# Causal attention in a transformer block: the order of the key tiles, and on diagonal steps both scores and the mask first

## The chip, the cores and the metric

One core of one Trainium2 chip. The metric is the device time of one launch in microseconds (us), lower is better. The core's engines run their own instruction streams and meet at semaphores: TensorE (PE, with its weight loads shown apart as PEld), VectorE (DVE), ScalarE (ACT), GpSimd (POOL) and SyncE (SP), which issues most of the DMAs.

## The reference, cut to what matters

Two batches of 2048 rows of 512 numbers pass a pre-norm block: attention with 16 heads of width 32 over a latent of 128, then a mixture of experts. Only the attention core is touched:

```python
scores = jnp.einsum('bhqd,bhkd->bhqk', q, k) / jnp.sqrt(jnp.float32(DH))
causal = jnp.tril(jnp.ones((s, s), dtype=bool))
scores = jnp.where(causal[None, None], scores, -jnp.inf)
attn = jax.nn.softmax(scores, axis=-1)
out = jnp.einsum('bhqk,bhkd->bhqd', attn, v)
```

## The kernel before, in words

Six phases follow each other: projections, attention, output projection with the shared expert, routing, experts, and combination. `phase_attention` is the one that changes.

**Units and steps.** Eight iterations (two batches, four groups of four heads) each have four units, one for each query chunk q = 0 to 3 of 512 queries. A unit goes through its key tiles kt of 128 keys: tiles below 4q are full, tiles 4q to 4q+3 lie on the diagonal, where tile number d = kt - 4q concerns only the queries from 128d on (512, 384, 256 and 128 columns). Each tile takes two steps, p = 0 and p = 1, for two head pairs. So there are 640 steps, 256 of them diagonal.

**A step on PE.** A step n computes two scores (keys x queries, one for each head of the pair, `score(n, 0)` and `score(n, 1)`) into a ring of three PSUM banks: score number i waits for the exponential of number i-3. On full tiles both exponentials wait only for their score. On diagonal tiles VectorE first adds a triangle to 128 columns of both scores (`mask(n)`), and both exponentials wait for that mask. In odd steps PE also multiplies the exponentials of an earlier tile with the values (`values`, four matmuls side by side, one and a half steps behind); in even steps, for some tiles, it adds up the exponentials with a matrix of ones (`count_ones`, two tiles behind). For the other tiles (`POOL_TILES`) GpSimd adds them up instead, and `finish` brings its sum into PSUM two or four steps into the next unit.

**The maxima.** The softmax subtracts a maximum of each row, which has to be known before the unit's first score. So for coming units PE computes scores the other way round, one *item* (a matmul into one of three other PSUM banks), VectorE takes its maximum, and when a unit's maxima are all there PE transposes them ("turn"), ScalarE copies the rows and SP's DMA puts them beside the queries. 1280 such items are laid over the steps by `attention_plan`: each step gets "room" for the PE work that the planner counts in it, and items are handed out in proportion. A step's items fall into three parts (`item_shares`). The order within a step before the change:

| engine | order in step n |
|---|---|
| PE | score(n,0), first third of the items, ones or values, second third, score(n,1), last third, finish |
| DVE | maxima of the first two thirds, mask(n), maxima of the last third |
| ACT | turn rows if any, exp(n,0), exp(n,1), output and sums of the unit before |

Each engine takes its stream strictly in this written order; PE therefore stands still where the next matmul in its stream has to wait.

Of the kernel before, what the change touches and what calls it, by code (L numbers as in the profile page):

```python
# [21 lines left out]
TPC = CH // P  # L22
# [337 lines left out]
NG = BATCH * GPB  # L360
HG = 4
PAIRS = 2
NQ = SEQ // CH
SCALE = 1.0 / DH ** 0.5


POOL_TILES = ((), (0, 1, 2, 4, 5), (0, 1, 2, 4, 5, 7, 8), (0, 1, 2, 4, 5, 7, 8, 10, 11, 12))
FINISH = (2, 4, 4, 2)
KRING = 6


def attention_steps():

    units = [(it, q) for it in range(NG) for q in range(NQ)]
    steps, first_step = [], []
    for u, (it, q) in enumerate(units):
        first_step.append(len(steps))
        steps += [(u, q, kt, p) for kt in range(TPC * (q + 1)) for p in range(PAIRS)]
    first_step.append(len(steps))
    return units, steps, first_step  # L380


def key_chunk_before(it, j):
# [5 lines left out]
def attention_plan(units, steps, first_step):  # L389

    stream, pending, turn_at = [], None, {}
    for u, (it, q) in enumerate(units):
        items = [("max", u, t, h, c) for t in range(TPC) for h in range(HG) for c in range(q + 1)]
        lag = 4
        stream += items[:lag]
        if pending is not None:
            turn_at[pending] = len(stream)
            stream.append(("turn", pending))
        stream += items[lag:]
        pending = u  # L400
    turn_at[pending] = len(stream)
    stream.append(("turn", pending))

    def cost(item):
        if item[0] == "turn":
            return 500
        _, u, t, h, c = item
        return 150 + min(CH, (TPC * units[u][1] + t + 1) * P - c * CH)

    def room(n):  # L410
        u, q, kt, p = steps[n]
        width = CH - max(kt - TPC * q, 0) * P
        work = 2 * max(width, 2 * P) + 100 * (kt >= TPC * q)
        if p:
            work += 4 * width
        elif kt not in POOL_TILES[q]:
            work += 4 * width
        return work

    costs = [cost(i) for i in stream]  # L420
    total = [0]
    for x in costs:
        total.append(total[-1] + x)
    rooms = [0]
    for n in range(len(steps)):
        rooms.append(rooms[-1] + room(n))

    released = []
    for u, (it, q) in enumerate(units):
        at = 0  # L430
        if it:
            at = first_step[u - NQ + 1] + 5
            kb = key_chunk_before(it, q)
            if kb is not None:
                at = max(at, first_step[NQ * kb[0] + NQ - 1] + 2 * TPC * (kb[1] + 1) + 5)
        released.append(at)
    due = [max(first_step[u] - 6, 0) for u in range(len(units))]
    start = turn_at[0] + 1
    upto, pos = [], start
    for n in range(len(steps)):  # L440
        slope = 0.0
        for u in range(len(units)):
            if turn_at[u] >= pos:
                slope = max(slope, (total[turn_at[u] + 1] - total[pos]) / max(rooms[due[u]] - rooms[n], 1400))
        upto_cost = slope * (rooms[n + 1] - rooms[n]) + (total[pos] if n == 0 else carry)
        while pos < len(stream) and total[pos] + costs[pos] / 2 < upto_cost:
            if stream[pos][0] == "max" and released[stream[pos][1]] > n:
                upto_cost = total[pos]
                break
            pos += 1  # L450
        carry = upto_cost
        upto.append(pos)
    turn_step = {}
    for n in range(len(steps)):
        for i in range(upto[n - 1] if n else start, upto[n]):
            if stream[i][0] == "turn":
                turn_step[stream[i][1]] = n
    for u in range(1, len(units)):
        assert turn_step[u] < first_step[u], (u, turn_step[u], first_step[u])
    return stream, start, upto, turn_at, turn_step  # L460
# [38 lines left out]
def phase_attention(nc, x, w, scratch, ahead):  # L499
# [37 lines left out]
    def pool_count(n):  # L537

        u, q, kt, p = steps[n]
        if kt == POOL_TILES[q][0]:  # L540
            n += PAIRS * (POOL_TILES[q][1] - POOL_TILES[q][0])
        return pool_ops.index(n) + 1

    def pool_total(u):
# [22 lines left out]
    with ExitStack() as ctx:  # L567
# [52 lines left out]
        with nc.Block() as block:  # L620
            @block.gpsimd
            def _(g):
# [11 lines left out]
                for i, n in enumerate(pool_ops):  # L634
                    u, q, kt, p = steps[n]
                    f = summed.index(u)
                    out = acc[f % 2][:, 2 * p:2 * p + 2]
                    lo = max(kt - TPC * q, 0) * P
                    so_far = out
                    if kt == POOL_TILES[q][1]:  # L640
                        so_far = pt[(n - PAIRS * (kt - POOL_TILES[q][0])) % NPB][:]
                        if f >= 2:
                            g.wait_ge(s_fin, f - 1)
                    else:
                        g.wait_ge(s_add, i - 1)
                    g.wait_ge(s_exp, 2 * n + 2)
                    if kt == POOL_TILES[q][1]:
                        assert lo == 0
                    g.tensor_tensor(out[:, :, lo:], so_far[:, :, lo:], pt[n % NPB][:, :, lo:], ALU.add).then_inc(s_add, 1)  # L649

            @block.sync
            def _(sp):
# [55 lines left out]
                for n in range(NS):  # L708
                    u, q, kt, p = steps[n]
                    it = units[u][0]  # L710
                    if n and kt == 0 and p == 0:
                        jt, j = units[u - 1]
                        if jt + 1 < NG:
                            sp.wait_ge(s_st, 2 * n)
                            load_q(jt + 1, j)
                        later = NQ * jt + j + KRING
                        if j == NQ - 1 and later < NG * NQ:
                            load_k(*divmod(later, NQ))
                    if q == NQ - 1 and kt % TPC == 0 and p == 0 and kt:
                        later = NQ * it + kt // TPC - 1 + KRING  # L720
                        if later < NG * NQ:
                            sp.wait_ge(s_st, 2 * n)
                            load_k(*divmod(later, NQ))
                    for s in range(NU):
                        if turn_step.get(s) == n:
                            turn_rows(s)
                    at = n - 4
                    if at >= 0:
                        vu, vq, vkt, vp = steps[at]
                        if vq == NQ - 1 and vkt % TPC == TPC - 1 and vp and units[vu][0] + 1 < NG:  # L730
                            sp.wait_ge(s_pv, (at + 1) // 2)
                            load_v(units[vu][0] + 1, vkt // TPC)
                    done = unit_ending(n, 3)
                    if done is not None:
                        store_out(done)
# [26 lines left out]
            def _(v):  # L762
# [36 lines left out]
                        ins.then_inc(s_msk, 1)  # L799

                for n in range(NS):
                    here, _, some, there = item_shares(n)
                    for i in range(here, some):
                        if stream[i][0] == "max":
                            partial_max(i)
                    if steps[n][2] >= TPC * steps[n][1]:
                        mask(n)
                    for i in range(some, there):
                        if stream[i][0] == "max":
                            partial_max(i)  # L810
                    if n == first_step[NQ * NG - 2]:
# [59 lines left out]
            def _(pe):  # L871
# [27 lines left out]
                def score(n, j):  # L899
# [3 lines left out]
                    lo = min(max(d, 0) * P, 2 * P)  # L903
                    if 2 * n + j >= NST:
                        pe.wait_ge(s_exp, 2 * n + j - NST + 1)
                    if kt == 0 and p == 0 and j == 0:
                        pe.wait_ge(s_row[q], 16 * (it + 1))
                    at = key_slot(it, kt // TPC) * CH + kt % TPC * P
                    h = 2 * p + j
# [3 lines left out]
                def values(m):  # L913
# [1 line left out]
                    it = units[u][0]  # L915
                    lo = max(kt - TPC * q, 0) * P
                    pe.wait_ge(s_exp, 4 * m + 4)
                    if kt == 0 and u:
                        pe.wait_ge(s_oev, u)
                    if q == kt // TPC and kt % TPC == 0:  # L920
                        pe.wait_ge(s_v[q], 16 * (it + 1))
                    for h in range(HG):
                        ins = pe.matmul(ob[h * DH:(h + 1) * DH, lo:], vbuf[:, kt, h * DH:(h + 1) * DH],  # L923
                                        pt[(2 * m + h // 2) % NPB][:, h % 2, lo:],
                                        start=(kt == 0), stop=(kt == TPC * q + TPC - 1))
                    ins.then_inc(s_pv, 1)

                def count_ones(m):
# [1 line left out]
                    if kt in POOL_TILES[q]:  # L930
                        return
                    lo = max(kt - TPC * q, 0) * P
                    begin = min(k for k in range(TPC * (q + 1)) if k not in POOL_TILES[q])
                    if kt == begin and u:
                        pe.wait_ge(s_sev, u)
                    for h in range(HG):
                        ins = pe.matmul(sb[h * DH:(h + 1) * DH, lo:], ones[:],  # L937
                                        pt[(2 * m + h // 2) % NPB][:, h % 2, lo:],
                                        start=(kt == begin), stop=(kt == TPC * q + TPC - 1 and not POOL_TILES[q]))
                    ins.then_inc(s_one, 1)  # L940

                def finish(u):
# [10 lines left out]

                for n in range(NS):
                    here, *some = item_shares(n)
                    score(n, 0)
                    for i in range(here, some[0]):
                        item(i)
                    if n % 2 == 0 and n >= 4:
# [2 lines left out]
                        values((n - 3) // 2)  # L962
                    for i in range(some[0], some[1]):
                        item(i)
                    score(n, 1)
                    for i in range(some[1], some[2]):
                        item(i)
                    done = unit_ending(n, FINISH)
# [942 lines left out]
```

## Time and profile before

| | |
|---|---|
| time, median of 3 runs | 2658.76 us (2655.09 to 2663.19) |
| the profiled execution | 2654.73 us, its span 2652.8 us |
| attention steps, first score to last exponential | 296 to 1486 us of the span |
| PE, weight loads, DVE, ACT, POOL busy over the span | 2338.7, 1478.8, 1560.3, 1053.6, 999.8 us |
| mean granted TensorE clock | 0.935 of full speed |

Busy time of an engine is the union of its instructions. The end of a matmul is modelled, so the PE is called busy for a while after it could take the next. "PEclk" in a row is the granted share of full clock in that stretch.

### The profile page before, as it was taken

The page shows a single profiled execution, that of the slowest core. Times are in us where ns is not written, and L with a number is a line of the kernel's source. Part 1 is how long each engine was busy: PE and PEld are TensorE (multiplying, and loading weights), DVE is VectorE, ACT ScalarE, POOL GpSimd, SP SyncE. Part 2 cuts the span into 40 slices and gives each one's busy share as a digit, 9 for nine tenths or more (in the row PEclk, how much of TensorE's full clock was granted, in tenths as well). Part 3 has the DMA queues.
Part 4 walks back from the last instruction along what each step waited for, and adds up shares of the span by engine and source line. Part 5 has one row for each costly group of instructions (what it writes and reads, how often), then busy time and mean ns, then how long its engine had stood idle before and what let it go on. Part 6 is the DMA issues. An engine that isn't in the chain of part 4 may idle for free. (4 is left out here: it accounts for less than half of the span.)

```text
span 2652.8 us, 34530 instructions
## 1 busy us (share of the span) xinstructions
PE 2338.7 (88%) x12088; PEld 1478.8 (56%) x12088; DVE 1560.3 (59%) x3220; ACT 1053.6 (40%) x1928; POOL 999.8 (38%) x592
## 2 busy tenths in 40 slices
PE   5997699999999999999999699999489999999950
PEld 5775344444444444444443377776467777777740
DVE  3664787667676777766674444443645555555535
ACT  2332155565555555555656422221033333333310
POOL 0000067474656566573746633130221111112036
PEclk8998599899999999998999899999589999999975
DMA  3766512213131313322110234341245454545349
GB/s 100 279 234 231 124 28 65 65 49 74 39 81 33 82 31 80 102 65 65 49 47 27 63 105 143 111 143 48 69 151 178 139 171 146 167 154 160 113 157 381
DMA packets 178740, 301.72 MB, mean 114 GB/s; under 512 B 23616, under 2 KB 65728, under 8 KB 178624
## 3 DMA queue, kind: packets, MB, share of 16 engines
q1 hardware_dynamic: 159360, 242.54, 30.1%
q0 software_dynamic: 14656, 49.29, 5.9%
q10 hardware_dynamic: 4608, 8.39, 0.8%
q8 instruction: 66, 1.08, 0.2%
q14 instruction: 50, 0.41, 0.1%
HBM read 199.65 MB, written 100.27 MB: 113 GB/s over the span
## 5 line engine op out<-in xcount | busy, mean ns | idle before, releaser
L832 ACT ACTIVATE b_pt<-b_st 128x512 f32<-128x512 f32 (+3 forms) x1280 | 620.8, 533 | 489.3 <-PE b_st L910 208.3
L773 DVE TENSOR_REDUCE b_mpart<-b_mx 128x1 f32<-128x512 f32 x768 | 510.2, 685 | 209.2 <-PE b_mx L889 207.4
L649 POOL TENSOR_TENSOR b_acc<-b_acc,b_pt 128x1024 f32<-128x1024 f32 (+1 forms) x256 | 593.4, 2344 | 73.3 <-ACT b_pt L832 73.0
L910 PE MATMUL b_st<-b_q,b_k 97*128 97x512 f32 (+2 forms) x1280 | 497.9, 405 | 71.9 <-ACT b_pt L832 57.9
L889 PE MATMUL b_mx<-b_k,b_q 96*128 96x512 f32 (+2 forms) x1280 | 514.5, 418 | 30.7 <-DVE b_mt L781 25.9
L889 PEld LDWEIGHTS b_mx<-b_k,b_q 96*128 96x128 f32 x1280 | 250.4, 197 | 306.7 <-DVE b_mpart L773 138.6
L910 PEld LDWEIGHTS b_st<-b_q,b_k 97*128 97x128 f32 x1280 | 244.2, 193 | 262.9 <-ACT b_pt L832 228.7
L923 PE MATMUL b_ob<-b_pt,b_v 128*32 128x512 f32 (+3 forms) x2560 | 305.7, 550 | 1.1 <-ACT b_pt L832 1.1
L770 DVE CUSTOM_DVE_ANT_0 b_unread<-b_mx,b_later 128x384 bf16<-128x384 f32 (+3 forms) x512 | 244.6, 483 | 77.9 <-PE b_mx L889 77.4
L649 POOL TENSOR_TENSOR b_acc<-b_pt 128x1024 f32<-128x1024 f32 x48 | 113.4, 2378 | 443.8 <-ACT b_pt L832 443.7
L61 PE MATMUL e_fb<-e_xh,e_w_guh 128*128 128x512 f32 (+1 forms) x552 | 219.6, 398 | 1.5 <-DVE e_xl L1730 1.5
L63 PE MATMUL e_fb<-e_xl,e_w_guh 128*128 128x512 f32 (+1 forms) x552 | 217.5, 394 | 0.0
L62 PE MATMUL e_fb<-e_xh,e_w_gul 128*128 128x512 f32 (+1 forms) x552 | 217.3, 394 | 0.0
L1702 ACT ACTIVATE e_sg<-e_fb 128x512 f32<-128x512 f32 (+1 forms) x69 | 41.1, 596 | 341.2 <-PE e_fb L63 341.2
L1674 POOL COPY e_idx<-token 128x4 uint32 (+1 forms) x23 | 4.2, 184 | 410.9 <-PE e_tb L1764 410.9
L1735 DVE TENSOR_TENSOR e_hf<-e_sg,e_fb 128x512 f32<-128x512 f32 (+1 forms) x69 | 47.3, 686 | 189.1 <-ACT e_sg L1702 189.1
L794 DVE TENSOR_TENSOR b_st<-b_st,b_sooner 128x256 f32<-128x256 f32 x170 | 72.9, 429 | 80.8 <-PE b_st L910 79.3
L937 PE MATMUL b_sb<-b_pt,b_ones 128*32 128x512 f32 (+3 forms) x1152 | 117.2, 481 | 0.0
L63 PEld LDWEIGHTS e_fb<-e_xl,e_w_guh 128*128 128x128 f32 (+1 forms) x552 | 98.8, 179 | 29.5
L61 PEld LDWEIGHTS e_fb<-e_xh,e_w_guh 128*128 128x128 f32 (+1 forms) x552 | 98.9, 179 | 29.2 <-issue 1.8
L1677 POOL DMA_INDIRECT e_xg<-scr_xn,e_idx x92 | 100.1, 1088 | 39.8 <-issue 21.0
L62 PEld LDWEIGHTS e_fb<-e_xh,e_w_gul 128*128 128x128 f32 (+1 forms) x552 | 98.8, 179 | 27.8
(224 smaller groups left out, 3524.2 us busy)
## 6 DMA issues: line engine op xcount, KB each, us to landing
scr_y<-e_y SPq DMA_DIRECT2D x23, 1024.0 KB, 5.0
b_q<-scr_qh SPq DMA_DIRECT2D x64, 256.0 KB, 4.4
b_k<-scr_kh SPq DMA_DIRECT2D x64, 256.0 KB, 4.0
e_gu<-in_L_ffn_w_gate_dram SPq DMA_DIRECT2D x23, 704.0 KB, 6.4
e_gu<-in_L_ffn_w_up_dram SPq DMA_DIRECT2D x23, 704.0 KB, 7.7
e_d<-in_L_ffn_w_down_dram SPq DMA_DIRECT2D x23, 512.0 KB, 7.7
a_xin<-in_L_attn_x_dram POOLq DMA_DIRECT2D x8, 1024.0 KB, 5.9
scr_qh<-a_qh SPq DMA_DIRECT2D x8, 1024.0 KB, 4.6
```

Source lines behind the costliest of these rows:

```text
L61: nc.tensor.matmul(out, wh, xh, start=first, stop=False)
L62: nc.tensor.matmul(out, wl, xh, start=False, stop=False)
L63: return nc.tensor.matmul(out, wh, xl, start=False, stop=last)
L649: g.tensor_tensor(out[:, :, lo:], so_far[:, :, lo:], pt[n % NPB][:, :, lo:], ALU.add).then_inc(s_add, 1)
L770: v.tensor_tensor_reduce(unread[i % NMX][:, 0:w], mxb[i % NMX][:, 0:w], later[:, CH - w:], 1.0, -3e38, ALU.add, ALU.max, part).then_inc(s_ ...
L773: v.tensor_reduce(part, mxb[i % NMX][:, 0:w], AX.X, ALU.max).then_inc(s_red, 1)
L832: act.activation(pt[n % NPB][:, j, lo:], stb[:, (2 * n + j) % NST, lo:], ACT.Exp, scale=SCALE).then_inc(s_exp, 1)
L889: ins = pe.matmul(bank[:, 0:max(w, 2 * P)], qb[0:KR, h, q * CH + t * P:q * CH + (t + 1) * P], kb[0:KR, h, at:at + max(w, 2 * P)], start=Tr ...
L910: pe.matmul(stb[:, (2 * n + j) % NST, lo:], kb[:, h, at:at + P], qb[:, h, q * CH + lo:(q + 1) * CH], start=True, stop=True).then_inc(s_st, 1)
L923: ins = pe.matmul(ob[h * DH:(h + 1) * DH, lo:], vbuf[:, kt, h * DH:(h + 1) * DH], pt[(2 * m + h // 2) % NPB][:, h % 2, lo:], start=(kt == ...
L937: ins = pe.matmul(sb[h * DH:(h + 1) * DH, lo:], ones[:], pt[(2 * m + h // 2) % NPB][:, h % 2, lo:], start=(kt == begin), stop=(kt == TPC * ...
L1677: g.indirect_dma_start(out=xg[n][:, t, :], in_=scratch["xn"], out_offset=None, in_offset=bass.IndirectOffsetOnAxis(ap=idx[n][:, t:t + 1], ...
```

## The change: what it does

1. The diagonal tiles no longer stand at the end of a unit but are put between full ones, by a written list `ORDER`. Everything that asked for the first or last tile, or for the distance of two tiles, now asks for the place in that list. The tiles whose sums PE makes are listed in `ONES_TILES`; GpSimd still adds the same number of tiles in each unit, with the same widths.
2. SP's loads into the key and value buffers of a chunk are issued when the last tile of that chunk has been used in the new order (`steps_to_leave`: after steps 10, 20, 30 and 32 of a unit with q = 3, instead of 8, 16, 24 and 32).
3. On diagonal steps PE issues score(n,1) directly behind score(n,0), ahead of the items and of ones or values.
4. VectorE applies mask(n) ahead of all maxima of step n.

```diff
-POOL_TILES = ((), (0, 1, 2, 4, 5), (0, 1, 2, 4, 5, 7, 8), (0, 1, 2, 4, 5, 7, 8, 10, 11, 12))
+ORDER = ((0, 1, 2, 3), (0, 1, 4, 2, 5, 3, 6, 7), (0, 1, 2, 8, 3, 4, 9, 5, 6, 10, 7, 11),
+         (0, 1, 2, 12, 3, 4, 5, 13, 6, 7, 8, 14, 9, 10, 11, 15))
+ONES_TILES = ((0, 1, 2, 3), (2, 6, 7), (2, 9, 6, 10, 11), (2, 4, 13, 8, 14, 15))
+POOL_TILES = tuple(tuple(kt for kt in ORDER[q] if kt not in ONES_TILES[q]) for q in range(NQ))
...
-        steps += [(u, q, kt, p) for kt in range(TPC * (q + 1)) for p in range(PAIRS)]
+        steps += [(u, q, kt, p) for kt in ORDER[q] for p in range(PAIRS)]
...
+def steps_to_leave(j):
+    return PAIRS * (1 + max(ORDER[NQ - 1].index(kt) for kt in range(TPC * j, TPC * (j + 1))))
...
                 for n in range(NS):
-                    here, _, some, there = item_shares(n)
-                    for i in range(here, some):
-                        if stream[i][0] == "max":
-                            partial_max(i)
+                    here, _, _, there = item_shares(n)
                     if steps[n][2] >= TPC * steps[n][1]:
                         mask(n)
-                    for i in range(some, there):
+                    for i in range(here, there):
                         if stream[i][0] == "max":
                             partial_max(i)
...
                     here, *some = item_shares(n)
+                    diag = steps[n][2] >= TPC * steps[n][1]
                     score(n, 0)
+                    if diag:
+                        score(n, 1)
                     for i in range(here, some[0]):
                         item(i)
...
-                    score(n, 1)
+                    if not diag:
+                        score(n, 1)
```

## Rows read from the trace of the kernel before

**Rows 1.** Every engine, in the attention steps (lengths and busy us, count; clock; DMA)

```profile
296.00:1486.00 1190.00, 1123.01 (x6548) 517.47 (x6552) 811.88 (x2128) 663.32 (x1373) 705.84 (x304) 0.97 0.22 55
```

**Rows 2.** Iteration 4: q = 0, then full and diagonal stretch of q = 1, 2, 3

```profile
core 0: us, PE busy (x) PEld busy (x) DVE busy (x) ACT busy (x) POOL busy (x), PEclk, DMA share, GB/s
911.09:926.59 15.50, 14.75 (x104) 6.30 (x103) 11.82 (x31) 7.10 (x18) 0.00 (x0) 1.00 0.58 137
926.59:940.79 14.20, 13.62 (x86) 6.78 (x86) 9.12 (x23) 9.82 (x20) 7.31 (x4) 1.00 0.29 75
940.79:954.05 13.26, 11.43 (x71) 5.31 (x70) 10.56 (x26) 6.27 (x15) 10.42 (x5) 1.00 0.01 1
954.05:982.29 28.24, 28.24 (x162) 12.57 (x161) 19.45 (x42) 18.59 (x35) 19.93 (x9) 1.00 0.15 38
982.29:997.37 15.08, 13.30 (x86) 6.46 (x85) 10.69 (x42) 6.76 (x16) 8.35 (x4) 1.00 0.01 2
997.37:1041.61 44.24, 44.24 (x255) 20.41 (x255) 29.41 (x82) 28.40 (x53) 33.34 (x15) 1.00 0.29 73
1041.61:1055.60 13.99, 11.53 (x72) 5.43 (x70) 11.15 (x29) 6.27 (x15) 8.94 (x4) 1.00 0.34 76
```

**Rows 3.** The same columns: full stretch of q = 2 in iterations 1, 2 and 6

```profile
510.65:544.38 33.73, 33.73 (x162) 15.39 (x162) 20.32 (x43) 18.91 (x35) 19.93 (x9) 0.81 0.13 33
659.25:691.92 32.67, 32.67 (x163) 14.86 (x162) 20.31 (x42) 18.63 (x35) 19.92 (x9) 0.84 0.13 33
1242.49:1275.34 32.85, 32.85 (x163) 14.99 (x163) 20.23 (x42) 18.63 (x35) 19.92 (x9) 0.83 0.13 33
```

**Rows 4.** Waits in the attention steps (us in total, times, longest)

```profile
ACT b_pt L832 <- DVE b_st L794: 178.4, 153, 18.9
...
PE b_st L910 <- ACT b_pt L832: 57.9, 90, 1.3
```

**Rows 5.** Groups by shape (count | busy us, mean ns | idle before)

```profile
L773 DVE TENSOR_REDUCE b_mpart<-b_mx 128x1 f32<-128x512 f32 x768 | 510.2, 685 | 209.2 <-PE b_mx L889 207.4
L832 ACT ACTIVATE b_pt<-b_st 128x512 f32<-128x512 f32 x896 | 497.0, 599 | 300.3 <-PE b_st L910 208.3 <-DVE b_st L794 59.2 <-DVE b_st L798 23.6
...
L832 ACT ACTIVATE b_pt<-b_st 128x128 f32<-128x128 f32 x128 | 28.6, 275 | 56.7 <-DVE b_st L794 35.2 <-DVE b_st L798 20.1 <-PE b_sb L937 1.4
```

**Rows 6.** Timeline, iterations 2 and 3: narrow diagonal steps (start, length, instruction, idle before)

```profile
761.94 0.28 PE L910 MATMUL b_st<-b_q,b_k 97*128 97x256 f32 x1
...
762.75 0.42 DVE L794 TENSOR_TENSOR b_st<-b_st,b_sooner 128x256 f32<-128x256 f32 x1
...
763.72 0.39 PE L910 MATMUL b_st<-b_q,b_k 97*128 97x256 f32 x1 [0.42 <-ACT b_pt L832]
...
764.15 0.50 DVE L798 TENSOR_TENSOR b_st<-b_st,b_sooner 128x128 f32<-128x128 f32 x2 [0.51 <-PE b_st L910]
...
764.76 0.45 ACT L832 ACTIVATE b_pt<-b_st 128x128 f32<-128x128 f32 x2 [0.82 <-DVE b_st L798]
...
765.09 0.39 PE L910 MATMUL b_st<-b_q,b_k 97*128 97x256 f32 x1
...
765.86 0.64 PE L937 MATMUL b_sb<-b_pt,b_ones 128*32 128x256 f32 x8
...
766.43 0.19 PEld L889 LDWEIGHTS b_mx<-b_k,b_q 96*128 96x128 f32 x1 [0.41 <-issue]
```

**Rows 7.** Timeline, iteration 3: tile 12 and the start of tile 13

```profile
896.20 0.63 PE L910 MATMUL b_st<-b_q,b_k 97*128 97x512 f32 x2
...
896.99 0.43 DVE L794 TENSOR_TENSOR b_st<-b_st,b_sooner 128x256 f32<-128x256 f32 x1
...
897.59 1.06 PE L923 MATMUL b_ob<-b_pt,b_v 128*32 128x512 f32 x8
898.58 0.19 PEld L889 LDWEIGHTS b_mx<-b_k,b_q 96*128 96x128 f32 x1 [0.84 <-DVE b_mpart L773]
...
900.61 0.44 PE L910 MATMUL b_st<-b_q,b_k 97*128 97x384 f32 x1 [0.78 <-ACT b_pt L832]
```

More of the change, by code:

```diff
@@ L434, in attention_plan @@
             if kb is not None:
-                at = max(at, first_step[NQ * kb[0] + NQ - 1] + 2 * TPC * (kb[1] + 1) + 5)
+                at = max(at, first_step[NQ * kb[0] + NQ - 1] + steps_to_leave(kb[1]) + 5)
         released.append(at)
@@ L540, in pool_count @@
         if kt == POOL_TILES[q][0]:
-            n += PAIRS * (POOL_TILES[q][1] - POOL_TILES[q][0])
+            n += PAIRS * (ORDER[q].index(POOL_TILES[q][1]) - ORDER[q].index(POOL_TILES[q][0]))
         return pool_ops.index(n) + 1
@@ L640, in _ @@
                     if kt == POOL_TILES[q][1]:
-                        so_far = pt[(n - PAIRS * (kt - POOL_TILES[q][0])) % NPB][:]
+                        so_far = pt[(n - PAIRS * (ORDER[q].index(kt) - ORDER[q].index(POOL_TILES[q][0]))) % NPB][:]
                         if f >= 2:
@@ L710, in _ @@
                     it = units[u][0]
-                    if n and kt == 0 and p == 0:
+                    if n and n == first_step[u]:
                         jt, j = units[u - 1]
@@ L718, in _ @@
                             load_k(*divmod(later, NQ))
-                    if q == NQ - 1 and kt % TPC == 0 and p == 0 and kt:
-                        later = NQ * it + kt // TPC - 1 + KRING
-                        if later < NG * NQ:
+                    for j in range(NQ - 1):
+                        if q == NQ - 1 and n == first_step[u] + steps_to_leave(j) and NQ * it + j + KRING < NG * NQ:
                             sp.wait_ge(s_st, 2 * n)
-                            load_k(*divmod(later, NQ))
+                            load_k(*divmod(NQ * it + j + KRING, NQ))
                     for s in range(NU):
@@ L729, in _ @@
                         vu, vq, vkt, vp = steps[at]
-                        if vq == NQ - 1 and vkt % TPC == TPC - 1 and vp and units[vu][0] + 1 < NG:
-                            sp.wait_ge(s_pv, (at + 1) // 2)
-                            load_v(units[vu][0] + 1, vkt // TPC)
+                        for j in range(NQ):
+                            if vq == NQ - 1 and at + 1 == first_step[vu] + steps_to_leave(j) and units[vu][0] + 1 < NG:
+                                sp.wait_ge(s_pv, (at + 1) // 2)
+                                load_v(units[vu][0] + 1, j)
                     done = unit_ending(n, 3)
@@ L905, in score @@
                         pe.wait_ge(s_exp, 2 * n + j - NST + 1)
-                    if kt == 0 and p == 0 and j == 0:
+                    if n == first_step[u] and j == 0:
                         pe.wait_ge(s_row[q], 16 * (it + 1))
@@ L917, in values @@
                     pe.wait_ge(s_exp, 4 * m + 4)
-                    if kt == 0 and u:
+                    if kt == ORDER[q][0] and u:
                         pe.wait_ge(s_oev, u)
@@ L924, in values @@
                                         pt[(2 * m + h // 2) % NPB][:, h % 2, lo:],
-                                        start=(kt == 0), stop=(kt == TPC * q + TPC - 1))
+                                        start=(kt == ORDER[q][0]), stop=(kt == ORDER[q][-1]))
                     ins.then_inc(s_pv, 1)
@@ L932, in count_ones @@
                     lo = max(kt - TPC * q, 0) * P
-                    begin = min(k for k in range(TPC * (q + 1)) if k not in POOL_TILES[q])
+                    begin = ONES_TILES[q][0]
                     if kt == begin and u:
@@ L938, in count_ones @@
                                         pt[(2 * m + h // 2) % NPB][:, h % 2, lo:],
-                                        start=(kt == begin), stop=(kt == TPC * q + TPC - 1 and not POOL_TILES[q]))
+                                        start=(kt == begin), stop=(kt == ORDER[q][-1] and not POOL_TILES[q]))
                     ins.then_inc(s_one, 1)
```

## The prediction

> **What bounds the kernel now.** I read the busy shares of the attention steps first, then stretches of one iteration, then the waits, then the timeline inside single steps. Only the attention steps are touched: 1190 of the 2652.8 us of span [rows 1]. There PE is busy 1123 us, VectorE 812, GpSimd 706, ScalarE 663 [rows 1]: PE sets the pace, and its 67 us without work are the plain stock that a better order could give back. Iteration 4, undisturbed, shows where they lie [rows 2]: nothing in the full stretches of q = 2 and 3, 0.58 us in that of q = 1, 0.75 in q = 0, and 1.83, 1.78 and 2.46 us in the diagonal stretches. Diagonal tiles cost 3.3 to 3.8 us each there, full ones 3.5 to 3.7, though the diagonal ones are narrower. The waits say why: ScalarE waits 178 us for the mask on two score banks, and PE waits 57.9 us, in 90 places, for an exponential before a score [rows 4]. The rest of PE's idle time is mostly the 12 us before the first row of maxima arrives, and the change doesn't touch that.
>
> The Trainium skill (Trainium Kernel Development and Optimization, "Reading a trace") calls the busy time of matmuls a bad measure and that of weight loads a good one. By it the stock is larger than 67 us, since weight loads are busy 517 of 1190 us; no row says how much larger, and the sum below does not use it.
>
> **The chain behind one wait.** In a run of narrow diagonal steps it is seen bare [rows 6]: a second score starts at 763.72, the mask at 764.15, the exponential at 764.76, and the score that reuses the bank at 765.09. That is 1.37 us with an exponential of 0.28 us (128 columns), so 1.09 us plus the exponential. From 0.28 to 0.60 us for 128 and 512 columns [rows 5], in even steps, the chain is 1.37, 1.47, 1.58 and 1.69 us for d = 3, 2, 1, 0. It gets longer if VectorE is still at maxima (0.69 us each [rows 5]) when the scores come: score to mask is 0.43 us bare, 0.81 us in the pair 761.94 and 762.75 [rows 6], and 0.56 us for tile 12 (its second score 0.23 us behind 896.20) [rows 7]. I take 0.35 us on top wherever a full tile with three items stands ahead; bounds are 0 and one maximum, 0.69.
>
> **Where the wait stands, before and after.** Between score(n,1) and score(n+1,1) PE has work that covers the chain. Before, from p = 0 to p = 1 that work holds the values, 1.0 us (897.59 to 898.58 [rows 7]), and the chain is hidden; from p = 1 to the next tile's p = 0 it holds only the next score and one or two items at 0.25 us, and PE stands (0.78 us at 900.61 [rows 7]), except where ones fall into that step. After, both scores stand at the head. From p = 1 onward the values follow them, and a full tile comes next: hidden. But from p = 0 to p = 1 there remain only the items of p = 0 and the next score. So the wait isn't removed, it changes places: one per diagonal tile.
>
> **The sum for a diagonal tile after**: own score issue (0.23, 0.18, 0.12, 0.12 us by width; 0.23 us apart in [rows 7], narrower ones in proportion) twice, the chain, the items of p = 1 at 0.25, and the values at 1.0, since a full tile's values now fall there. The planner's own costs and rooms, gone through by hand for the new order, give p = 1 of the diagonal tiles 3, 2, 1, 1 items for q = 1 and 3 and 2, 2, 3, 1 for q = 2.
> - q = 3: 0.23 + 2.04 + 0.23 + 0.75 + 1.0 = 4.25 for d = 0; 3.79, 3.31 and 3.21 for d = 1, 2, 3: 14.6 us, against 13.99.
> - q = 2: 4.0 + 3.79 + 3.81 + 3.21 = 14.8, against 15.08.
> - q = 1: 4.25 + 3.79 + 3.31 + 2.43 = 13.8, against 13.26 (tile 7 follows tile 6, so its chain is bare and its values take 0.57 us, as the 256 columns of 765.86 to 766.43 [rows 6]).
> Together 43.2 against 42.3 us [rows 2]: +0.8 us an iteration.
>
> What moves to the full stretches: values of diagonal tiles, narrower by 0.65 us (q = 2, 3) and 0.2 us (q = 1), -1.5; ones, +0.35, +1.8 and +1.0, since tile 2 and most ones of diagonal tiles now run there, less 1.15 that leaves the first steps of the next unit; some three items from the diagonal stretch of q = 2, +0.85. That is +1.3 us. With the diagonal part +2.1 us an iteration, +17 us over eight. The last unit has no items, so neither backlog nor cover; I leave it as the others.
>
> **q = 0** keeps its order, all steps diagonal; only parts 3 and 4 act. 15.5 us with VectorE 11.8 busy [rows 2]. Tiles 0 and 1 stay near VectorE's work and `finish`, tiles 2 and 3 go down to the chain: 0.8 us a unit, seven units, -6 us. The first unit's burst of items is VectorE's either way.
>
> **The clock.** Three full stretches of q = 2 take 33.7, 32.7 and 32.9 us at a granted clock of 0.81 to 0.84, against 28.24 at 1.00 in iteration 4 [rows 2, 3]. Parts of them ran at 1.2 instead of 2.4 GHz; that costs 14.5 us in all, and each follows q = 1's diagonal stretch, where PE has idled. After, q = 1's tiles 6 and 7 still stand together with two waits of about 1 us. I count -4; bounds are -15 (no dip left) and +23 (a dip in all eight). By the Trainium skill (TensorE: Matmul & The Clock Gate, "The HAM clock gate") idleness drops the clock to half and sustained work brings it back; the trace agrees as to the order of events.
>
> **What costs nothing.** GpSimd adds as many tiles, equally wide. In q = 3 its last run of three (9, 10, 11) starts some 17 us before `finish` (four tiles of 3.6 us, then a tile of the next unit) and takes six additions of 2.4 us (33.34 us in 15 records of the full stretch [rows 2]), 14.3 us: hidden by some 3 us; uncovered it would cost up to 3 us in each iteration. SP's chunk loads start 2 to 6 steps later, 4 to 11 us, are used in the next iteration, and nothing urgent is queued behind them: the row DMA of step 17 lies between those of steps 10 and 20. The two row turns that move one step later (q = 1 and 3) still precede their unit by more than 10 us. The masks number the same; behind a waiting mask on VectorE stand that step's maxima, behind those PE's items three banks on. VectorE, at 11.15 of 13.99 us [rows 2], has room.
>
> **Sum**: 2654.7 (profiled) + 17 - 6 - 4 = 2661.7. The median of the runs is 4.0 us above the profiled execution, so about **2666 us**.
>
> **Rivals.**
> - *The masks get in at once.* The 0.35 us goes for some 80 tiles (-28), and with spread waits the dips go too (-11): 2627. For: VectorE takes no maximum ahead of the mask any more, and only 0.13 us of delay shows at tile 12 [rows 7]. Against: the previous p = 1 step issues its last item just ahead of the diagonal scores.
> - *VectorE becomes late*, the other mechanism that ends slower. Waiting in line for two scores at every mask, it loses about 0.45 us a step of p = 0 and 1 (192 steps outside q = 0), while two or three items wait behind. It decides once VectorE's 11.15 us plus eight such waits, 3.6, exceed the stretch's 14.6: just there. If half of it reaches PE, +43: 2709.
> - *More clock dips.* One wait per tile in q = 1 after the rows' turn leaves PE idle in a third of the tiles; dips in all units would give 2666 + 27 = 2693. Against: full stretches between waits have no idle time at all.
>
> **How the numbers follow.** Likeliest, 0.48: the waits change places, 2645 to 2685. Masks at once, 0.27: 2605 to 2645. VectorE late, 0.15: 2685 to 2730. Clock, 0.10: 2675 to 2700. No change means within 0.3%, 2650.8 to 2666.7. The likeliest case splits into 0.09 faster, 0.25 same, 0.14 slower. So faster 0.36, same 0.25, slower 0.39. For 8 in 10: 2618 to 2702.
>
> **What would show it.** The wait of PE's scores for exponentials: about 88 times, longest at d = 0 (about 1.2 us), all in front of p = 1's second score, none in full tiles. Diagonal tiles of q = 3 at 4.2, 3.8, 3.3 and 3.2 us. If the score-to-mask time is 0.43 in p = 0, the first rival holds; if PE's items wait for maxima in diagonal tiles, the second. The prediction is wrong if the diagonal tiles of an iteration lose over 3 us together: then the cover I counted from the values and ones is larger than it is, or the backlog of maxima smaller.

## The result and the profile after

The changed kernel takes 2709.65 us (median of 4 runs, 2701.75 to 2711.5) against 2660.98 us for the kernel before: a ratio of 1.0175, 95% interval 1.0146 to 1.0205. It is slower by 48.7 us. The forecast was 2666 us, with 2618 to 2702 as its range.

The attention steps after the change, the row that answers to [rows 1]:

```profile
296.00:1526.00 1230.00, 1140.59 (x6542) 523.40 (x6540) 816.38 (x2127) 671.29 (x1372) 700.63 (x302) 0.96 0.21 53
```

Both rows start at 296 us, but the first score stands at 294.53 us here and at 296.51 us before. From there to the last exponential the steps take 1231.8 us instead of 1189.1: 43 us more. PE idles 89 us in the row instead of 67. Every engine executes as many instructions as before, but PE is also busy 18 us longer with them. The granted clock (0.96 for 0.97) goes with that; by the clock records of the two traces PE ran at the lower of its two levels, 1.2 instead of 2.4 GHz, for 91 us of the attention steps, and for 70 before.

By iteration, from first score to first score (the last one to the last exponential), with the granted clock of that stretch (the third kernel is the first of the experiments):

| iteration | 0 | 1 | 2 | 3 | 4 | 5 | 6 | 7 |
|---|---|---|---|---|---|---|---|---|
| before, us | 170.0 | 149.4 | 149.3 | 145.8 | 144.5 | 143.1 | 149.8 | 137.0 |
| its clock | 0.92 | 0.95 | 0.97 | 0.99 | 1.00 | 1.00 | 0.95 | 0.99 |
| changed, us | 183.8 | 151.1 | 148.5 | 150.0 | 155.5 | 148.9 | 151.9 | 141.9 |
| its clock | 0.88 | 0.98 | 1.00 | 0.99 | 0.95 | 1.00 | 0.98 | 0.95 |
| tile order alone, us | 174.2 | 143.7 | 143.6 | 143.7 | 143.7 | 145.1 | 144.3 | 138.9 |
| its clock | 0.90 | 1.00 | 1.00 | 1.00 | 1.00 | 0.99 | 1.00 | 0.95 |

So an iteration at full clock loses 4.0 to 5.8 us, and iteration 0 alone, with its long stretch at the lower clock, loses 14.

The span grew by 47.3 us, from 2652.8 to 2700.1. The attention starts 2 us earlier and lasts 42.7 us longer, so 6.6 us lie behind it, where no line was changed. 4.2 of them are a wait that the tile order makes. The last unit has no unit behind it, so its `finish` runs straight after the last tile, and GpSimd now adds tile 11 just ahead of tile 15. PE waits for that sum; in the changed kernel and then before:

```profile
1531.79 1.94 PE L950 MATMUL b_sb<-b_acc,b_ones 128*32 128x512 f32 x8 [4.81 <-POOL b_acc L657]
```

```profile
1486.92 1.95 PE L945 MATMUL b_sb<-b_acc,b_ones 128*32 128x512 f32 x8
```

From the last exponential to this matmul it is 5.5 us instead of 1.35. The inner order alone, whose tile order is the old one, has 0.95 us there, and the tile order alone has 4.64. What makes the other 2.4 us stays open; behind this matmul the profiled executions of the kernels here differ by up to 6 us among themselves.

Where PE waits, as in [rows 4], to the end of the attention steps; the third row is PE waiting for a maximum:

```profile
ACT b_pt L837 <- DVE b_st L802: 152.9, 163, 12.0
...
PE b_st L915 <- ACT b_pt L837: 83.0, 123, 1.8
...
PE b_mx L894 <- DVE b_mpart L781: 3.4, 8, 1.9
```

PE's scores wait 83 us for exponentials, 123 times, against 57.9 us and 90 times [rows 4]. Sorted by place, 65 us of it in 86 places stand in front of the second score of p = 1 in diagonal tiles of q = 1 to 3, 8 us in 8 places in front of p = 0's there, 7.5 us in 22 places in q = 0, and 2 us in other places. PE hardly ever waits for a maximum.

Iteration 5 after the change, undisturbed at full clock, in the columns of [rows 2]: q = 0, 1, 2, 3.

```profile
1083.57:1099.13 15.56, 14.47 (x96) 6.30 (x97) 12.38 (x31) 6.79 (x17) 3.35 (x2) 1.00 0.94 205
1099.13:1128.34 29.21, 25.73 (x154) 12.06 (x154) 19.44 (x48) 16.71 (x36) 17.70 (x8) 1.00 0.47 138
1128.34:1174.43 46.09, 42.25 (x255) 19.67 (x255) 31.43 (x85) 25.99 (x53) 27.70 (x12) 1.00 0.09 25
1174.43:1232.50 58.07, 55.59 (x323) 26.09 (x324) 39.61 (x107) 34.73 (x69) 39.64 (x18) 1.00 0.26 64
```

Against [rows 2] (15.50; 14.20 + 13.26 = 27.46; 43.32; 58.23) q = 0 and q = 3 are unchanged; q = 1 loses 1.75 us and q = 2 loses 2.8. Against the same iteration of the kernel before, also at full clock (15.57, 27.41, 42.83, 57.32 us), they lose 0, 1.8, 3.3 and 0.75 us. The diagonal tiles themselves, in the order 4, 5, 6, 7, then 8, 9, 10, 11, then 12, 13, 14, 15, with their sum:

```profile
1106.03:1110.51 4.48, 3.62 (x18) 1.43 (x17) 2.93 (x8) 3.11 (x7) 4.48 (x3) 1.00 1.12 296
1114.39:1118.22 3.83, 3.00 (x17) 1.39 (x16) 2.32 (x6) 2.16 (x5) 2.05 (x2) 1.00 0.00 0
1122.14:1125.44 3.30, 2.73 (x17) 1.21 (x15) 2.93 (x8) 1.51 (x4) 3.30 (x2) 1.00 0.00 0
1125.44:1128.34 2.90, 1.86 (x15) 1.07 (x15) 1.79 (x5) 0.86 (x5) 0.18 (x1) 1.00 0.00 0
1139.80:1143.99 4.19, 3.11 (x17) 1.40 (x15) 2.56 (x7) 2.37 (x5) 1.19 (x1) 1.00 0.00 0
1151.27:1155.30 4.03, 3.10 (x18) 1.52 (x17) 3.23 (x8) 2.16 (x5) 4.03 (x3) 1.00 0.00 0
1162.90:1167.48 4.58, 2.93 (x20) 1.48 (x18) 1.95 (x11) 2.89 (x7) 0.00 (x0) 1.00 0.01 2
1171.09:1174.43 3.34, 3.16 (x24) 1.28 (x22) 2.60 (x8) 1.49 (x5) 3.34 (x2) 1.00 0.02 7
1185.39:1189.80 4.41, 3.46 (x19) 1.62 (x18) 2.88 (x10) 2.73 (x5) 1.55 (x1) 1.00 0.00 0
1200.25:1204.22 3.97, 3.97 (x24) 1.48 (x23) 2.89 (x9) 1.79 (x4) 3.61 (x2) 1.00 0.02 4
1215.22:1218.65 3.43, 2.65 (x17) 1.25 (x15) 2.79 (x8) 1.70 (x5) 0.53 (x1) 1.00 0.51 130
1229.10:1232.50 3.40, 2.65 (x16) 1.14 (x15) 2.56 (x7) 1.49 (x5) 3.40 (x2) 1.00 0.61 148
sum 45.86, PE 36.25 PEld 16.27 DVE 31.43 ACT 24.25 POOL 27.67; mean PE 3.02 PEld 1.36 DVE 2.62 ACT 2.02 POOL 2.31
```

The reader sees PE idle 0.6 to 1.65 us in ten of the twelve diagonal tiles. In tile 13, in whose p = 0 step 1.0 us of ones (those of tile 4) falls, PE never idles, and in tile 11, which has the narrower ones of tile 10 there, only 0.2 us. The worst is tile 10. Its timeline:

```profile
1162.50 0.68 PE L901 MATMUL b_mx<-b_ident,b_mt 128*97 128x128 f32 x4
...
1163.21 0.60 ACT L843 ACTIVATE b_rows<-b_mx 97x512 fp32r<-97x512 f32 x1 [2.37 <-PE b_mx L901]
1163.71 1.08 ACT L837 ACTIVATE b_pt<-b_st 128x512 f32<-128x512 f32 x2
...
1164.35 0.39 PE L915 MATMUL b_st<-b_q,b_k 97*128 97x256 f32 x1 [1.05 <-ACT b_pt L837]
...
1165.82 0.39 PE L915 MATMUL b_st<-b_q,b_k 97*128 97x256 f32 x1 [0.60 <-ACT b_pt L837]
```

(A line with `x2` or more merges neighbouring instructions.) The transposes of the row turn are the last item of the step before. ScalarE's row copy waits 2.37 us for them, and the two exponentials of that step, whose scores were long there, stand behind the copy. Tile 10's second score stands at the head of PE's stream and waits 1.05 us for the first of them. Then comes the wait from p = 0 to p = 1 as everywhere.

### The profile page after: what moved, and what is told of

It is laid out like the page before. It is cut to its first block and busy times, and to the rows that moved or that the text cites. A ratio compares the mean times of both kernels' runs of the same rounds, so it can differ in the third digit from the quotient of the medians.

```text
span 2700.1 us, 34529 instructions
## 1 busy us (share of the span) xinstructions
PE 2358.2 (87%) x12088; PEld 1485.8 (55%) x12088; DVE 1565.2 (58%) x3219; ACT 1062.0 (39%) x1928; POOL 1002.1 (37%) x592
## 3 DMA queue, kind: packets, MB, share of 16 engines
q8 instruction: 66, 1.08, 0.2%
## 5 line engine op out<-in xcount | busy, mean ns | idle before, releaser
L837 ACT ACTIVATE b_pt<-b_st 128x512 f32<-128x512 f32 (+3 forms) x1280 | 628.2, 533 | 510.0 <-PE b_st L915 264.6
L915 PE MATMUL b_st<-b_q,b_k 97*128 97x512 f32 (+2 forms) x1280 | 483.9, 404 | 95.1 <-ACT b_pt L837 83.0
L894 PE MATMUL b_mx<-b_k,b_q 96*128 96x512 f32 (+2 forms) x1280 | 501.9, 422 | 30.3 <-DVE b_mt L789 25.9
L894 PEld LDWEIGHTS b_mx<-b_k,b_q 96*128 96x128 f32 x1280 | 242.7, 197 | 339.9 <-DVE b_mpart L781 153.4
```

What stands on the lines that cost most here:

```text
L837: act.activation(pt[n % NPB][:, j, lo:], stb[:, (2 * n + j) % NST, lo:], ACT.Exp, scale=SCALE).then_inc(s_exp, 1)
L894: ins = pe.matmul(bank[:, 0:max(w, 2 * P)], qb[0:KR, h, q * CH + t * P:q * CH + (t + 1) * P], kb[0:KR, h, at:at + max(w, 2 * P)], start=Tr ...
L915: pe.matmul(stb[:, (2 * n + j) % NST, lo:], kb[:, h, at:at + P], qb[:, h, q * CH + lo:(q + 1) * CH], start=True, stop=True).then_inc(s_st, 1)
```

## The experiments

Times are medians; the ratio is to the kernel before, run beside them, with its 95% interval.

| kernel | us | ratio |
|---|---|---|
| changed kernel | 2709.65 | 1.0175 (1.0146 to 1.0205) |
| tile order alone | 2646.17 | 0.9935 (0.9914 to 0.9956) |
| inner order alone | 2699.53 | 1.0139 (1.0113 to 1.0164) |
| changed, mask behind maxima | 2876.86 | 1.0795 (1.0766 to 1.0825) |
| changed, ones as cover | 2632.63 | 0.9889 (0.9865 to 0.9914) |
| changed, step behind the turn as of old | 2708.45 | 1.0173 (1.0140 to 1.0205) |
| order alone, ones as cover | 2638.51 | 0.9920 (0.9893 to 0.9947) |
| changed, inner order only at p = 0 | 2679.49 | 1.0083 (1.0054 to 1.0112) |
| changed, inner order only at p = 1 | 2782.45 | 1.0466 (1.0434 to 1.0497) |
| before, 4 score banks | 2691.99 | 1.0117 (1.0080 to 1.0153) |
| changed, 4 score banks | 2674.46 | 1.0065 (1.0038 to 1.0092) |
| ones as cover, old inner order in q = 1 | 2636.08 | 0.9911 (0.9884 to 0.9937) |
| changed, rows behind exponentials | 2690.26 | 1.0091 (1.0052 to 1.0130) |
| before, rows behind exponentials | 2663.71 | 1.0027 (0.9999 to 1.0056) |
| ones as cover, rows behind exponentials | 2608.58 | 0.9819 (0.9769 to 0.9869) |
| order alone, rows behind exponentials | 2643.22 | 0.9938 (0.9916 to 0.9960) |

**The two halves of the change.** Each alone: the inner order's lines of the diff are taken back for the first, the tile order's for the second.

> The new order of the key tiles alone; inside a diagonal step the second score and the mask stand where they stood before. Theory A (the inner order does the harm: with both scores at the head, the step from p = 0 to p = 1 has nothing to cover the mask's chain): the wait moves back to the places behind the values, and the 43 us of the attention steps are mostly gone: 2660 to 2675 us. Theory B (the tile order does the harm: ones and values of full width now fall beside diagonal tiles, and q = 2's row turn stands straight in front of tile 10): 2695 to 2710 us, little changed from the changed kernel.

> The old order of the key tiles, with both scores at the head of a diagonal step and the mask ahead of all maxima. Theory A: diagonal tiles get slower as in the changed kernel, 2690 to 2715 us. Theory B: the inner order is harmless or useful, 2650 to 2665 us, since the tiles' narrow steps follow each other as before. In q = 0, whose tile order never changed, this kernel and the changed one should agree under both.

The order alone is 16 us faster than the kernel before beside it; the inner order costs 37 us on the old tile order and 63 us on the new one. Theory A is right about which half does the harm; its time for the order alone, 2660 to 2675 us, was missed by 14 us on the fast side.

What the order alone gains is for the most part clock. At full clock its iterations take 143.6 to 143.7 us, no less than the 143.1 and 144.5 of the kernel before, and its scores wait 54.7 us for exponentials against 57.9. But its iterations 1 to 4 all run at full clock, and only 52 us of its attention steps are at the lower level, against 70. In [rows 3] some 34 us at the lower level cost 14.5 us, or 0.42 us each; by this estimate 18 us fewer are worth 7 to 8 us of the 11 us that separate the attention steps of the two profiled executions. The mean granted clock of all its executions, 0.938 against 0.932, points the same way. Tiles 12, 13, 14 and 15 with the tile order alone, iteration 5:

```profile
1148.85:1152.05 3.20, 3.20 (x19) 1.63 (x17) 2.69 (x9) 1.69 (x3) 0.33 (x1) 1.00 0.00 0
1162.45:1166.26 3.81, 3.81 (x25) 1.46 (x23) 2.49 (x7) 1.47 (x3) 3.62 (x2) 1.00 0.01 3
1178.21:1181.09 2.88, 2.49 (x17) 1.30 (x15) 2.35 (x7) 1.26 (x3) 0.69 (x1) 1.00 0.62 154
1191.48:1193.87 2.39, 2.39 (x16) 1.07 (x15) 2.12 (x6) 1.04 (x3) 2.39 (x2) 1.00 0.49 137
```

12.28 us where the changed kernel takes 15.21. Not all of that is gained: with a late second score the wait falls into the full tile behind, and the whole unit takes 56.67 us against 58.07.

**Where the mask stands.** `mask(n)` goes back behind two thirds of the maxima.

> The changed kernel with the mask back behind two thirds of the step's maxima; both scores stay at the head. If the mask's place matters by itself (a maximum of 0.69 us delays it), each diagonal step of two or three items gets about 0.7 us later: 2740 to 2780 us. If VectorE's waiting in line for the scores is what costs, as the second rival of the prediction has it, this kernel is faster than the changed one: 2680 to 2700 us.

167 us slower than the changed kernel, and 97 us above the highest time expected. PE's scores wait 170 us for exponentials, in 178 places. The other outcome, that the kernel gets faster once VectorE no longer waits in line for the scores, did not come; with the scores early, the mask has to be early too.

**The inner order at p = 0 or p = 1 only.** In the same steps alone the mask stands ahead of the maxima; that part of the edit is not shown.

```diff
-                    diag = steps[n][2] >= TPC * steps[n][1]
+                    diag = steps[n][2] >= TPC * steps[n][1] and steps[n][3] == 0   # or == 1
```

> The changed kernel with the new inner order only in diagonal steps with p = 0; p = 1 keeps the old one. Between the second scores of p = 0 and p = 1 there are now items, a score, and the values of 1.0 us. If the bare gap from p = 0 to p = 1 is the cause, it is covered and the time is that of the tile order alone or a little under, 2638 to 2652 us. If an early mask is harmful by itself (VectorE waiting in line), it stays above 2680 us.

> The changed kernel with the new inner order only in diagonal steps with p = 1; p = 0 keeps the old one. The second score of p = 0 is now issued late in its step and that of p = 1 at once, so the gap is even barer: if the gap is the cause, as slow as the changed kernel or slower, 2705 to 2740 us. If an early mask at p = 0 were the harm, it would come down to 2650 to 2680 us.

With only p = 1 early the kernel takes 2782.45 us, 42 us more than the highest time expected. Tiles 13 and 14 of iteration 5 come to 4.77 and 4.03 us, from 3.97 and 3.43 in the changed kernel:

```profile
1263.70:1268.47 4.77, 4.05 (x24) 1.47 (x23) 2.98 (x9) 2.09 (x5) 3.60 (x2) 1.00 0.01 2
1279.47:1283.50 4.03, 2.65 (x17) 1.33 (x16) 2.79 (x8) 1.71 (x5) 0.51 (x1) 1.00 0.44 116
```

That is the barest gap: a late second score followed by an early one. It also lengthens q = 0, to 20.1 us in iteration 5. With p = 0 early the expected time was missed by 27 us. In q = 1 to 3 the gap is covered (26.8, 43.9 and 56.3 us in iteration 5), but in q = 0, where all tiles are diagonal, the late second score of p = 1 is now followed by the early one of the next tile: the unit takes 19.36 us, against 15.56.

```profile
1063.64:1083.00 19.36, 14.74 (x97) 6.33 (x97) 12.56 (x31) 7.21 (x18) 4.29 (x2) 1.00 0.94 215
```

**Covering the gap with ones.** `ONES_TILES` is chosen so that PE's ones run between the two second scores.

```diff
-ONES_TILES = ((0, 1, 2, 3), (2, 6, 7), (2, 9, 6, 10, 11), (2, 4, 13, 8, 14, 15))
+ONES_TILES = ((0, 1, 2, 3), (0, 4, 5), (1, 3, 5, 10, 11), (1, 4, 7, 10, 14, 15))
```

> The changed kernel with the tiles whose sums PE makes chosen two places ahead of the diagonal ones, so that 1.0 us of ones stands between the second scores of p = 0 and p = 1: ones for (0, 4, 5), (1, 3, 5, 10, 11) and (1, 4, 7, 10, 14, 15) in q = 1, 2, 3. If the cover of the chain is the cause, each covered diagonal tile loses its wait of about 1 us, 3 tiles more in q = 3, 3 in q = 2, 3 in q = 1, against 0.9 us more of ones in q = 1 and 0.2 in q = 2: some 7 us an iteration, 2650 to 2665 us. If the wait is not the cause, PE's added ones make it 9 us slower, about 2718 us.

> The tile order alone (inner order as before), with PE's ones placed so that they run in the step p = 0 behind each diagonal tile, where the order alone leaves its wait: ones for (1, 2, 6), (2, 4, 6, 10, 11) and (2, 5, 8, 11, 14, 15). Four more diagonal tiles of an iteration are covered, 0.9 us each, against 1.1 us of wider ones: 2.5 us an iteration, 2620 to 2632 us. If waits behind p = 1 aren't what is left in the order-alone kernel, the wider ones cost 9 us: about 2655 us.

77 us off the changed kernel, 30 under the one before beside it, though PE computes more. That is 17 us less than the lowest time expected. An iteration at full clock takes 141.4 us against 148.9, the 7 us that were expected; the rest goes at least in part with the clock, since only 46 us of the attention steps are at the lower level against 91. PE's waits for exponentials fall to

```profile
PE b_st L915 <- ACT b_pt L837: 37.2, 73, 1.5
```

On the order alone, the same idea gives 8 us of the 14 to 26 expected. Taking the old inner order in q = 1 again gave nothing more (2636.08 us, where 2612 to 2632 were expected):

> The new tile order; in q = 0, 2 and 3 the new inner order with PE's ones two places ahead of the diagonal tiles, and in q = 1 the old inner order with the changed kernel's ones (2, 6, 7). From the units' own times in the runs so far: 15.1 + 27.0 + 42.6 + 55.1 = 139.8 us an iteration, against 141.3 with the ones' cover everywhere (2633 us): 2620 us, between 2612 and 2632. If the units depend on their neighbours' order more than on their own, no better than 2633 us.

**Another bank for the scores.** `NPB, NST, NMX = 8, 4, 2`: a score then waits for the exponential four scores back.

> The kernel before with four banks for the scores and two for the maxima instead of three and three. A score then waits for the exponential four scores back, so score(n+1,1) no longer needs the exponential of its own tile's step n, 0. Theory (the chain over the ring of three is what makes PE stand): its 58 us of waits for exponentials nearly vanish; what two banks for the maxima cost is not known from a row, bounds 0 and one PE stop of 0.3 us for each of 1280 items, so 2600 to 2900 us; this run is the base of the next.

> The changed kernel with four score banks and two for the maxima. Theory: with the chain out of PE's way the inner order costs nothing, and this kernel is within 10 us of the before kernel with the same banks, or under it, where the two stood 49 us apart with three banks. Rival (VectorE waiting in line at each mask, or the wider ones, cost the time): the difference of 40 to 50 us stays.

The order of the two turns round: the changed kernel is 17.5 us faster than the one before; its iterations 1 to 6 take 144.4 to 146.9 us against 147.7 to 150.4. Its waits for exponentials are gone, and those for maxima, with two banks, have grown. They have grown as much in the kernel before, so the comparison is even in them; the first row is that kernel's:

```profile
PE b_mx L889 <- DVE b_mpart L773: 31.6, 97, 3.2
PE b_mx L889 <- DVE b_mpart L770: 5.9, 23, 0.5
```

```profile
PE b_mx L894 <- DVE b_mpart L781: 37.4, 108, 3.1
...
PE b_st L915 <- ACT b_pt L837: 1.6, 3, 0.9
```

So the loss needs the ring's chain: with the same tile order, the same ones and the same mask first, nothing is lost once a score waits for an exponential further back. What the inner order costs or gives by itself with four banks stays open, as the tile order alone was not run with them.

**The row turn in front of tile 10.** First the step behind the turn keeps its old inner order (edit not shown), then ScalarE copies the rows behind the exponentials:

```diff
-                    for u in range(NU):
-                        if turn_step.get(u) == n:
-                            copy_rows(u)
                     exps(n)
+                    for u in range(NU):
+                        if turn_step.get(u) == n:
+                            copy_rows(u)
```

> The changed kernel, but the one step of an iteration that follows q = 2's row turn directly (tile 10, p = 0) keeps the old inner order: second score behind two thirds of the items, mask behind two thirds of the maxima. In the changed kernel PE idles 1.05 us there, since the exponentials of the step before stand behind the row copy on ScalarE, and the clock often falls next. Theory: this place costs its own 1 to 2 us an iteration and some of the clock's dips: 2692 to 2702 us. Rival: the items and their maxima ahead only move the wait to the second score of p = 1: 2706 to 2713 us.

> The changed kernel with ScalarE's row copy behind the two exponentials of its step instead of ahead of them. In q = 2 the turn is the last item of step 17, and tile 10's second score of p = 0 stands at the head of step 18 waiting for an exponential behind that copy; PE idles 1.05 us. Theory: that wait and a part of tile 10's excess go, 1 to 1.6 us an iteration, 2696 to 2702 us. Rival: the copy is not what holds the exponential, or it only moves on as when the step kept its old inner order: 2706 to 2713 us.

> The kernel before, with ScalarE's row copy behind the exponentials of its step. In the changed kernel that move took 19 us off. If those are particular to it (the turn of q = 2 right in front of a diagonal step whose second score stands at the head), the kernel before gains under a third of them: 2654 to 2664 us. If holding the exponentials behind the copy costs wherever a turn stands, it gains as much: 2640 to 2648 us.

> The tile order alone, old inner order, with the row copy behind the exponentials. Here tile 10's second score stands behind two items, and its two steps take 1.93 + 1.78 us. If the 19 us need the score at the head, the gain is under 6 us: 2640 to 2648 us. If the copy hurts at any place, 2628 to 2636 us.

> The changed kernel with both mendings, the ones two places ahead of the diagonal tiles and the row copy behind the exponentials. In the ones' cover kernel tile 10 still takes 2.98 + 1.73 us, of which about 1 us is the copy. If the two losses are separate and add up: 2633 - 8 to -16, 2617 to 2625 us. If the ones already cover what the copy delays, no change: 2629 to 2636 us.

Taking back the inner order of that one step gives nothing: PE still waits 0.93 and 0.60 us in tile 10, which takes 4.58 us as before. Moving the copy takes 19 us off the changed kernel, more than the 8 to 14 expected, and tile 10 falls from 4.58 to 3.26 us:

```profile
1158.67:1161.93 3.26, 2.53 (x20) 1.35 (x18) 1.95 (x11) 2.10 (x6) 0.00 (x0) 1.00 0.01 3
```

But the wait isn't gone, most of it changes places. The copy also frees the bank that held the transposed rows, and a later item waits for that bank:

```profile
PE b_mx L894 <- ACT b_rows L843: 7.8, 9, 1.1
```

Such a wait was not there before the move, and the scores' waits fell by 8.5 us, from 83.0 to 74.5. Tile 1 of q = 3 takes 5.16 us in iteration 2 where it took 3.84, so an iteration at full clock still takes 148.2 to 148.3 us, against 148.5 and 148.9. What has gone is the clock's fall: in the changed kernel it falls while tile 10 runs in five of the eight iterations, and here in one. Only 72 us of the attention steps are at the lower level, for 91, an estimated 8 us of the 15 that the attention steps lose in the profiled executions; the mean granted clock of all executions is 0.937 for 0.929. With the step behind the turn as of old, tile 10 kept its waits and the clock fell there in five iterations as well.

On the kernel before the move gains nothing: its scores' waits fall from 57.9 to 49.0 us and its items' waits for the copy grow from 0.8 to 12.9. On the tile order alone tile 10 gains 1.1 us and tile 1 of q = 3 loses 1.3; the clock fell in tile 10 in one of the eight iterations to begin with, and the time changes by 3 us. With the ones as cover the move takes off 24 us, more than the 8 to 16 expected. There only 1.1 us of waits for the copy appears, and an iteration at full clock falls from 141.4 to 138.8 us. The result is 2608.58 us, 2% under the kernel before, with 20 us of waits left:

```profile
PE b_st L915 <- ACT b_pt L837: 20.2, 50, 1.5
```

## Why the prediction was wrong

**Right.** PE paces the attention, and the mechanism was named: no cover from p = 0 to p = 1, a wait there for each diagonal tile (about 88 were forecast, 86 stand there), next to none in full tiles. q = 3 hardly changed (58.07 against 58.23 us in [rows 2] and 57.32 in the iteration after it). What moved to the full stretches: 148.93 - 45.86 - 15.56 = 87.5 us against 86.7 [rows 2], +0.8 where +1.3 was counted.

**The step that failed** is the sum for a diagonal tile: 43.2 us an iteration, measured 45.9, so +3.5 instead of +0.8 against [rows 2]. That is over the 3 us which the prediction gave as its own sign of being wrong. Over eight iterations it makes some 22 us. Three sizes in it were off.
- Tile 10 was set at 3.81 and took 4.58. The chain counted mask and exponential, but not what ScalarE has in its queue ahead of the exponential. The turn in front of tile 10 keeps its step, number 17 of q = 2, so it was not among the two that move and were looked at; new is that a score at the head of PE's stream stands behind it. The copy moved back takes 1.3 us off the tile.
- Tile 7 took 2.90 us, not 2.43. Its chain was taken as bare, but a maximum was in front of the mask in VectorE:

```profile
1125.88 0.69 DVE L781 TENSOR_REDUCE b_mpart<-b_mx 128x1 f32<-128x512 f32 x1 [0.81 <-PE b_mx L894]
...
1126.48 0.42 DVE L802 TENSOR_TENSOR b_st<-b_st,b_sooner 128x256 f32<-128x256 f32 x1
...
1127.35 0.39 PE L915 MATMUL b_st<-b_q,b_k 97*128 97x256 f32 x1 [1.04 <-ACT b_pt L837]
```

- The tiles with d = 0 took 4.48, 4.19 and 4.41, not 4.25, 4.0 and 4.25, and tiles 9, 11, 13, 14 and 15 each 0.1 to 0.25 more. Why was not taken apart.

**q = 0** was to gain 0.8 us a unit and gained nothing (15.56 against 15.50 us): 6 us over seven units.

**The clock** was to give back 4 us. Instead PE ran at the lower level for 21 us more of the attention steps, which at 0.42 us each is an estimated 9 us lost. The gain was expected in the full stretches of q = 2, and there the clock did fall less; but in five iterations it fell in tile 10, right behind the wait that the sum did not have. The executions differ in this, and the profiled one of the changed kernel is the fastest of its four.

**GpSimd's sum** was called hidden, and it is, except behind the last unit, where no unit follows: 4.8 us of PE's time.

**All together.** The four differences, 22, 6, 13 and 4 us, less 4 us by which the full stretches were counted too dear, make 41 us, by an estimate that scales one iteration up. The profiled execution is 40 us above the 2661.7 us of the sum.

**The framing hid the size of it.** "The wait changes places" was true of the count and false as a price. The tile order alone gains 16 us, by the estimate above mostly in clock, and the inner order loses 63 us on top. Two effects of opposite sign were added into one number near zero, and neither was priced alone.

**A reading.** The prediction put the rest of PE's idle time down to the 12 us before the first row of maxima arrives. That wait ends at 296.51 us, so nearly all of it lies ahead of the row of [rows 1], which starts at 296. Nothing in the sum hangs on it.

**The rivals.** VectorE late (2709 us) has the measured time by its number but not by its mechanism: PE waits 3.4 us for maxima in all. That its number fits is chance. Masks at once is refuted by the time, 83 us above its 2627, and tile 7 above shows a mask behind a maximum. More clock dips is borne out in part, with the estimated 9 us above; but in iterations at full clock the loss of 4.0 to 5.8 us is there without any.

## What to carry to other kernels

In a ring of banks, price the wait by what the waiting engine has to do between two uses of one bank, and do it for each neighbour pair. Here a late issue followed by an early one, with nothing long between them, was the worst (p = 1 early alone, and p = 0 early alone in q = 0), while early followed by late was covered. An operation put at the head of an in-order stream waits for everything in its producer's queue, so look there for the rare instruction (here a row copy) that stands ahead; and before moving it, look at what waits for that instruction, for the wait may only move there. Where a change has two parts, price each alone before adding them. Work that must be done anyway (the ones) is best placed where the chain needs cover. Compare the same stretch at the same granted clock first, and count the clock apart.

## What the runs showed of the hardware that was not expected

**Short waits went with falls of the clock.** In the changed kernel PE stands still for 1.05 us in tile 10 of every iteration, and in iterations 1, 3, 4, 6 and 7 the granted clock went to the lower level 0.9 to 1.6 us behind the end of that wait, for 3.4 to 6.8 us. In iterations 0, 2 and 5, with the same wait, it did not, nor did it in tile 8, which has a wait of 1.08 us in iteration 2. Without the wait in tile 10 (rows behind exponentials) it fell there in one iteration of eight. By the Trainium skill (TensorE: Matmul & The Clock Gate, "The HAM clock gate") the gate follows how busy TensorE was just before. These two kernels agree with that; what decides between two iterations with the same waits, no run here shows.

**What a fall costs.** The same 46 us unit, q = 2 of the changed kernel, takes 46.1 us in iteration 5 and 53.2 us in iteration 4, where the clock fell twice, for 10.2 and 6.8 us.

```profile
928.04:1083.57 155.53, 145.21 (x825) 66.56 (x826) 102.98 (x268) 84.49 (x173) 88.41 (x39) 0.95 0.23 55
1083.57:1232.50 148.93, 138.03 (x825) 64.13 (x826) 102.86 (x271) 84.21 (x172) 88.39 (x39) 1.00 0.32 81
```

PE's records number the same in both iterations, and it is busy 7.2 us longer in the first.
